# Mamba stage: delta products that contract over 128 rows, the last 112 of them zero in the weights

## The reference

```python
x_dbl = jnp.einsum('bld,rd->blr', ut, x_proj_w)          # 512 features -> 48
dt_low = x_dbl[..., :DT_RANK]                            # the first 16 of them
B_var = x_dbl[..., DT_RANK:DT_RANK + D_STATE]            # 16
C_var = x_dbl[..., DT_RANK + D_STATE:]                   # 16
delta = jax.nn.softplus(jnp.einsum('blr,dr->bld', dt_low, dt_proj_w) + dt_proj_b)
dA = jnp.exp(delta[..., None] * A)
dBu = delta[..., None] * B_var[:, :, None, :] * ut[..., None]
h = da * h + dbu                                         # scan over the 2048 tokens
y = jnp.einsum('bdn,bn->bd', h, c)
```

## Time and profile before

| | before |
|---|---|
| time, median of 3 runs | 4417.06 us (4415.48 to 4420.0) |
| the profiled execution's own time | 4411.45 us |
| its span, first to last instruction | 4409.7 us |
| mean granted TensorE clock over the span | 0.910 of 2.4 GHz |
| busy: PE / DVE / ACT / POOL | 3621.9 / 3809.4 / 3450.5 / 3471.0 us |

### The profile page before, as it was taken

How to read it: one execution, slowest core, us unless ns; L and a number is a source line. 1 busy time by engine, 2 the same in 40 slices (tenths; PEclk the granted TensorE clock), 3 DMA queues, 4 the chain that set the end, 5 groups by cost and what they waited for, 6 DMA issues and landing times. The chain is left out here.

```text
span 4409.7 us, 57988 instructions
## 1 busy us (share of the span) xinstructions
PE 3621.9 (82%) x19574; PEld 2535.3 (57%) x19574; DVE 3809.4 (86%) x4906; ACT 3450.5 (78%) x5856; POOL 3471.0 (79%) x1757
## 2 busy tenths in 40 slices
PE   8788888888888888888888888888865499999990
PEld 3455555555555555555555555555554388888880
DVE  5999999999999999999999999999995665665545
ACT  6888988898888888888888988888871265565656
POOL 3889989999899999999989999999882255555533
PEclk9899999999999999999999999999976699999995
DMA  2566666666666666666666666666652133333328
GB/s 85 137 153 163 155 152 154 162 154 157 153 150 157 152 153 162 156 157 152 167 146 158 149 153 154 152 158 154 153 133 48 59 73 64 61 62 64 64 30 309
DMA packets 179621, 592.74 MB, mean 134 GB/s; under 512 B 33392, under 2 KB 99056, under 8 KB 128128
## 3 DMA queue, kind: packets, MB, share of 16 engines
q0 software_dynamic: 70080, 332.96, 39.1%
q1 hardware_dynamic: 104640, 239.32, 15.7%
q10 hardware_dynamic: 4608, 16.78, 0.9%
HBM read 221.47 MB, written 68.68 MB: 66 GB/s over the span
## 5 line engine op out<-in xcount | busy, mean ns | idle before, releaser
L436 POOL TENSOR_TENSOR dbu<-du,bb 128x2048 f32<-128x2048 f32 x511 | 2397.1, 4726 | 202.7 <-DVE h L849 178.8
L849 DVE TENSOR_TENSOR_SCAN h<-da,hlast,dbu 128x512 f32<-128x512 f32 x1536 | 1873.7, 1264 | 27.6 <-POOL dbu L436 20.8
L492 ACT ACTIVATE da<-dl,negA 128x512 f32<-128x512 f32 x2048 | 1397.3, 693 | 216.6 <-DVE h L849 214.0
L742 PE MATMUL ht<-ident,h 128*128 128x128 f32 x8192 | 1216.8, 297 | 349.0 <-ACT pair L511 178.6
L742 PEld LDWEIGHTS ht<-ident,h 128*128 128x128 f32 x8192 | 1014.7, 153 | 761.3 <-DVE h L849 320.0
L849 DVE TENSOR_TENSOR_SCAN h<-da,dbu 128x512 f32<-128x512 f32 x512 | 593.5, 1203 | 11.6 <-ACT da L492 7.4
L511 ACT ACTIVATE pair<-ht,ct 128x512 f32<-128x512 f32 x768 | 512.0, 681 | 86.7 <-PE ht L742 84.3
L666 PE MATMUL spare<-xin,win 128*128 128x512 f32 x1024 | 491.8, 610 | 9.1 <-DMA xin<-in_xt 7.5
L675 PE MATMUL spare<-xh,conv 128*128 128x512 f32 x1024 | 463.4, 595 | 0.8 <-ACT xh L523 0.8
L857 DVE SCALAR_TENSOR_TENSOR pair<-ht,ct,pair 128x512 f32<-128x512 f32 x544 | 393.4, 728 | 50.7 <-PE ht L742 50.6
L1410 ACT ACTIVATE hraw<-f,b 128x512 f32<-128x512 f32 x256 | 176.3, 689 | 260.8 <-PE f L1468 244.9
(11 more groups left out here) (183 smaller groups left out, 5576.6 us busy)
## 6 DMA issues: line engine op xcount, KB each, us to landing
acc<-pair POOLq DMA_DIRECT2D x190, 1024.0 KB, 7.3
bb<-b_rows SPq DMA_DIRECT2D x128, 1024.0 KB, 5.1
acc<-acc POOLq DMA_DIRECT2D x64, 1024.0 KB, 8.6
dl<-du POOLq DMA_DIRECT2D x62, 512.0 KB, 7.7
xin<-in_xt SPq DMA_DIRECT2D x32, 512.0 KB, 8.4
xres<-in_x SPq DMA_DIRECT2D x32, 512.0 KB, 8.7
x_scores<-xres SPq DMA_DIRECT2D x32, 512.0 KB, 3.0
sums<-xres SPq DMA_DIRECT2D x32, 512.0 KB, 4.0
```

The lines of the kernel that those rows point to most:

```text
L436: pool.tensor_tensor(dbu[n % 2][:], du[q][:], bb[part % 2][:, m:m + 1, :].to_broadcast([P, DT, CH]), ALU.mult).then_inc(dbu_done, 1)
L492: act.activation(da[DA_SLOT[m]][:], dl[q][:, dt, :], ACT.Exp, scale=negA[:, dt, n:n + 1]).then_inc(exp_done, 1)
L742: last = te.transpose(ht[HT_SLOT[m]][:, dt * P:(dt + 1) * P], h[n % 2][:, dt, b * P:(b + 1) * P], ident[:])
L849: dve.tensor_tensor_scan(h[n % 2][:, dt, :], da[DA_SLOT[n * DT + dt]][:], dbu[n % 2][:, dt, :], start, ALU.mult, ALU.add).then_inc(scan_do ...
```

## The change

The tile `wdt` gets 128 partitions, and so does `xdbl`. POOL clears both once at the start, ahead of everything else it does there. The load of `wdt` fills its first 16 rows, and ACT's copy the first 48 of `xdbl`, as before; rows 16 to 127 of the weight and 48 to 127 of the moving tile stay zero. The D steps contract over all 128 rows. Rows 16 to 47 of `xdbl` hold B and C and meet zero weights, so the products are the same. SP waits for the first clearing before it issues the seven weight loads, and ACT for both before its first copy to `xdbl`. CT reads rows 0 to 47 by name.

```diff
-        wdt = a.sb("wdt", [16, 512])
+        wdt = a.sb("wdt", [P, 512])
+        wdt_rows = wdt[0:16]
...
-        xdbl = a.sb("xdbl", [48, CH])
+        xdbl = a.sb("xdbl", [P, CH])
...
+        padded = S("rows_padded")
...
                 load_xin(0, 0)
+                sp.wait_ge(padded, 1)
                 for dst, src in ((wconv, d["wconv"]), (vecs, d["vecs"]), (wx, d["wx"]), (negA, d["alog"]),
-                                 (wdt, d["wdt"]), (wo, d["wo"]), (gate, d["gate"])):
+                                 (wdt_rows, d["wdt"]), (wo, d["wo"]), (gate, d["gate"])):
...
             def _(pool):
+                pool.memset(wdt[:], 0.0).then_inc(padded, 1)
+                pool.memset(xdbl[:], 0.0).then_inc(padded, 1)
                 pool.memset(ident[:], 0.0).then_inc(ident_ok, 1)
...
-                        if not is_first(f):
+                        if is_first(f):
+                            act.wait_ge(padded, 2)
+                        else:
                             act.wait_ge(b_out, 16 * f)
-                        act.copy(xdbl[:], bank[0:48, :]).then_inc(done, 1)
+                        act.copy(xdbl[0:48, :], bank[0:48, :]).then_inc(done, 1)
...
-                            last = te.transpose(bank[:, b * 48:b * 48 + 48], xdbl[:, b * P:(b + 1) * P],
+                            last = te.transpose(bank[:, b * 48:b * 48 + 48], xdbl[0:48, b * P:(b + 1) * P],
                                                 ident[0:48, 0:48])
...
-                        last = te.matmul(bank[:], wdt[:, i * P:(i + 1) * P], xdbl[0:16, :],
+                        last = te.matmul(bank[:], wdt[:, i * P:(i + 1) * P], xdbl[:],
                                          start=True, stop=True)
```

## The result

| | before | after |
|---|---|---|
| time, median of 4 runs | 4416.27 us (4413.94 to 4420.0) | 4381.16 us (4376.85 to 4388.05) |
| ratio of the runs, 95% interval | | 0.9921 (0.9904 to 0.9938) |
| the profiled execution's span | 4409.7 us | 4378.4 us |
| mean granted clock over the span | 0.910 | 0.930 |

The account below looks back on a forecast made before the run. DVE was taken to set stage 1's pace. Of 38.8 us of its waits behind the D steps, 4 would stay, saving 35, with 0 for durations and start: 4417.06 - 35 = 4382 us, 80% range 4366 to 4412.

Parts of the forecast that it names:

- DVE sets the pace, and the loss is its wait behind D 1 and D 2: Stage 1: DVE waits 47.8 us for PE's turned blocks, 38.8 us of it behind the D steps.
- A matmul on few rows counts for little towards the clock, rows of zeros count: TensorE's clock: the number of rows addressed counts, zeros or not; 16 rows count for little.
- Durations unchanged: Delta products: 128 rows cost 0 to 8 ns a matmul, at most 1.0 us in all; taken as 0.
- The clock falls still, but rises sooner: D stretch: the clock can still fall ahead of D 1, but the four 128-row matmuls should raise it, one stretch sooner.
- 4 us in all for the chunks that begin a sequence: D stretch: short falls still cost something in half of the eight such chunks, about 4 us; elsewhere nothing.
- half of 0.95: Chunks that begin a sequence: a fall through D 1 and D 2 leaves 0.95 us of wait, in half of them.
- the 38.8 of the forecast: Stage 1: DVE's time lost behind the D steps, 81% of its 47.8 us of waits for turned blocks.
- the term for the D stretch: Waits behind the D steps: 38.8 us less 4 us that stay, so 35 us saved.
- the wait of 15 us or less: Sign in the changed kernel's profile: DVE's waits for `ht` at 15 us or less in place of 47.8.
- No change, by busy share alone: Rival for the clock: zeros don't count, or busy share alone rules; time stays 4417 within 0.2%; 13% together.
- Half of the gain lost to POOL: Rival in stage 1: the clock stays up, but a sooner DVE waits more for POOL's `dbu`; 4400 us; 8%.
- Dearer places: Rival: clock falls move to chunk starts, 2.3 us more each; with 25 of 31 chunks 4439 us; 5%.

Follow-up runs that it names:

- e3: The changed kernel with the delta products contracting over 96 rows in place of 128: 4402.26 us.
- e7: The changed kernel with delta products on 16 rows, and transpose step CT over 128 rows and columns, done three times: 4389.34 us.
- e1: The changed kernel, padded tiles and clearings kept, with delta products contracting over 16 rows again: 4411.96 us.
- e4: The changed kernel with ones in place of zeros in rows 48 to 127 of `xdbl`, against the same zero weights: 4379.07 us.
- e6: The changed kernel with transpose step CT over 128 rows and columns in place of 48 and 48, done three times: 4367.71 us.
- e5: The changed kernel with transpose step CT over 128 rows and columns in place of 48 and 48, done twice: 4375.02 us.

## Why the prediction was right, point by point

*DVE sets the pace, and the loss is its wait behind D 1 and D 2.* Right: the wait fell by 25.9 us, that for `dbu` by nothing, and every run in the table with a shorter wait for `ht` than e3's is faster than e3. Among them the order isn't kept: e7 waits less than the changed kernel and is slower, since it waits elsewhere.

*A matmul on few rows counts for little towards the clock, rows of zeros count.* Right, and shown by e1, the three kernels between 16 and 128 rows, and e4. Zeros in the weights' added rows are part of every kernel here.

*Durations unchanged.* The minimum grew by 5 ns; the bound was 8, and I took 0. By the same sum, 4 x 0.005 x 31, that is 0.6 us.

*The clock falls still, but rises sooner.* Right where it is seen at 513.37. What such a short fall costs was mis-sized. I had read it from one chunk, 1647.85 to 1651.20, where the fall began behind D 1 and D 2 and cost nothing, and took 4 us in all for the chunks that begin a sequence. (That chunk hasn't had exactly one short fall, as I wrote: it had another at 1627.40, the first line below.) But the pause lies ahead of D 1, so the fall mostly begins ahead of it and slows it too. The four chunks from 1671.7 to 2077.3 answer to the earlier trace rows, all four first, then the stretches at 1720, 1924 and 2026 (in the one at 1823 there was none):

```profile
1627.40:1630.70 3.30, 2.69 (x13) 2.69 (x14) 3.30 (x4) 3.27 (x5) 3.30 (x2) 0.50 1.10 221
...
DVE pair L864 <- PE ht L749: 3.3, 5, 1.8
...
DVE pair L864 <- PE ht L749: 1.8, 1, 1.8
...
DVE pair L864 <- PE ht L749: 0.3, 1, 0.3
...
DVE pair L864 <- PE ht L749: 0.5, 1, 0.5
```

2.6 us stay of 4.3, where I had expected half of 0.95. The longest was not in my bounds for one fall: at 1725 the clock fell ahead of D 1, PE began late in the slow stretch, and it took until behind the transposes before it rose. I then added up DVE's waits within 12 us of D 1's start over the whole stage. Before the change they come to 39.5 us, so that the 38.8 of the forecast was right. After it 11.2 stay: 6.9 in the eight chunks that begin a sequence, and 4.3 in the others, for which I had taken nothing. So the term for the D stretch was 28 us and not 35; the 4 us for what stays was the part that was wrong.

*Why the total agreed all the same.* Part of it was elsewhere. Between the profiled executions the span fell by 31.3 us. Since stage 1 is over sooner after the change, I count from DVE's first scan to its last: 3275.3 us before and 3244.2 after, 31.1 less. Of these, 27.2 are the wait for `ht` (the first line below; 21.9 after), 1.5 the wait for ACT, 0.9 idle time that the profile gives to nobody, and DVE's busy time is 1.9 less; waits that grew take back 0.9, and 0.5 stay without a row. The first scan came 0.9 us sooner (55.02 to 54.08), and what lies behind the last took 0.7 us longer. The prologue, for which I had counted nothing, was at half clock from 46 to 54 us, behind the delta products, and is at full clock now (the two stretches, before and after):

```profile
DVE pair L857 <- PE ht L742: 49.1, 49, 2.7
...
46.00:54.00 8.00, 6.38 (x9) 2.66 (x9) 7.17 (x12) 5.92 (x9) 0.00 (x0) 0.51 0.00 0
...
46.00:54.00 8.00, 6.34 (x14) 2.69 (x15) 7.38 (x13) 6.19 (x9) 0.00 (x0) 1.00 0.01 2
```

The other 3.8 to the 35.1 of the medians is spread: the changed kernel's runs lie between 4376.85 and 4388.05. That 35 was met within a microsecond is thus partly luck; the term for the wait was 7 to 8 us too large, and small gains and the spread made up for it. Of the signs that I had named, the wait of 15 us or less was missed with 21.9.

*The rivals.* No change, by busy share alone: ruled out by e1 against the changed kernel. Half of the gain lost to POOL: the wait for `dbu` is 24.6 where it was 24.4. Dearer places: six chunks of the changed kernel still have a fall in their first 5 us (seven before), and the waits for ACT and POOL didn't grow (9.1 us where it was 10.6, and 24.6 where it was 24.4). Most of the 2.3 us that I had taken for the price of such a fall isn't the fall's: the same chunk of the changed kernel, 2278.40 to 2382.20, has none in its first 57 us and takes 103.80 us all the same (it was 104.20):

```profile
2278.40:2335.40 57.00, 42.12 (x214) 25.31 (x212) 55.53 (x56) 52.21 (x88) 50.14 (x21) 1.00 0.53 135
2278.40:2382.20 103.80, 83.71 (x418) 54.36 (x416) 100.16 (x111) 91.32 (x157) 93.16 (x41) 0.97 0.63 152
```

The rule of the Trainium skill ("TensorE: Matmul & The Clock Gate", Part 1) that the clock follows how busy the PE is agrees with e6, where more work kept it up: the mean granted clock of its runs is 0.933 to 0.938, the changed kernel's 0.925 to 0.932. (e5's, 0.926 to 0.931, is no higher.) It isn't the whole of it: with 16 rows PE was busy for 3.39 of 3.41 us at clock 0.50 and the clock stayed down behind it, with 128 it was busy for 2.93 of 3.35 us at 512.95 and the clock was up behind it.

## What to carry to other kernels

A matmul that contracts over 16 rows ran no more than 5 ns faster than one over 128 (587 and 592 ns), and can hold TensorE at 1.2 GHz for the work behind it; padding with zero rows cost 5 ns a matmul here and took 0.8% off a kernel in which TensorE wasn't even the bound. Look for it where full matmuls behind small ones take twice their usual time and somebody waits for them. Work without use in a pause of TensorE can hold the clock too, but only where nobody waits for TensorE at that moment: the version with the highest clock was 11 us slower than the best.

## What the runs showed of the hardware

Rows counted neither in proportion nor in groups of 32: 16, 64, 96, 112 and 128 rows came out 5, 3, 15, 25 and 38 us below the kernel before. Rows of zeros on both sides were worth as much as ones against zero weights. The clock rose behind 16 transposes, which stream an identity (3.45 us at clock 0.50, then 1.00), and more transposes in a pause kept it up (e6). Runs of one kernel spread over 12 us (4409.51 to 4421.53 in 21 runs of the one before), so that one profiled execution tells a gain only to within some us.
